# Another order of the last four quarters, Pool scales two of them instead of three, and the row numbers come in two transfers

## The reference

```
x = layer_norm(dense_t @ Wd.T, gd, bd)                         # 2048 x 128
y = layer_norm(einsum('bnd,ed->bne', rows, Ws), gs, bs)        # 26 rows of each sample, 64 -> 128
y = einsum('bne,pn->bep', y, Wsi)                              # 26 features mixed to 32
y = layer_norm(y, gsi, bsi)                                    # over the 32
T = concatenate([x[:, None, :], swapaxes(y, 1, 2)], axis=1)    # 33 vectors of 128
Z = einsum('bnd,bmd->bnm', T, T)                               # all products, lower triangle kept
z = layer_norm(Z[:, tril] @ Wl.T, gl, bl)[:, :384]
h = concatenate([z, dense_t], axis=1)
h = maximum(h @ W_top1 + b_top1, 0)
h = maximum(h @ W_top2 + b_top2, 0)
out = h @ W_top3
```

## Time and profile before

| | us |
|---|---|
| median of 3 runs | 568.91 (567.0 to 570.04) |
| the profiled execution | 569.84 |
| its span, first to last instruction | 568.0 |
| PE busy | 507.3 (89%) |
| DVE busy | 396.6 (70%) |
| Pool busy | 402.7 (71%) |
| ACT busy | 292.3 (51%) |
| mean granted TensorE clock | 0.982 |

### The profile page before, as it was taken

The page is one execution under the profiler, slowest core; times in us unless marked ns, Lnnn a source line. Parts: engine busy times, 40 slices in busy tenths (PEclk is TensorE's granted clock), DMA queues, the critical chain, the costliest instruction groups (busy, mean ns, idle before and its releaser), DMA issues.

```text
span 568.0 us, 20126 instructions
## 1 busy us (share of the span) xinstructions
PE 507.3 (89%) x7271; PEld 380.6 (67%) x7271; DVE 396.6 (70%) x706; ACT 292.3 (51%) x758; POOL 402.7 (71%) x423
## 2 busy tenths in 40 slices
PE   1887869999999999999989899898989899997998
PEld 1854546767677767777676677677667676866576
DVE  4677975877676877768676787767676876675720
ACT  1434565546464655555454545555454654644543
POOL 5777777777777777777777777777777777776310
PEclk9979799999999999999999999999999999998999
DMA  7711221313121221313131221313131221313020
GB/s 250 265 31 28 59 59 30 91 28 93 28 81 39 70 53 28 93 27 92 31 92 28 70 51 35 85 31 91 29 90 32 67 52 29 93 28 90 1 67 2
DMA packets 32138, 36.06 MB, mean 63 GB/s; under 512 B 11789, under 2 KB 20950, under 8 KB 32038
## 3 DMA queue, kind: packets, MB, share of 16 engines
q0 software_dynamic: 13248, 13.65, 12.6%
q1 hardware_dynamic: 18790, 21.11, 11.4%
HBM read 25.54 MB, written 9.18 MB: 61 GB/s over the span
## 4 chain that ended last, share of the span: by engine, by line
POOL 51%; issue 21%; PE 12%; DVE 7%; DMA 4%; ACT 4%; DVEq 0%; ACTq 0%; POOLq 0%
POOL rows L656 51%; DMA rows<-in_table,ids_based 4%; PE bank_z L813 2%; PE bank_b L772 2%; DVE y L432 1%; PE bank_z L745 1%; DVE scaled L394 1%; DVE r_vec L458 1%; DVE y_var L442 1%; PE bank_d L856 1%; PE bank_z L792 1%; PE bank_z L739 1%; PE bank_z L719 1%; DVE scaled L419 1%; PE bank_aw L760 1%
## 5 line engine op out<-in xcount | busy, mean ns | idle before, releaser
L656 POOL DMA_INDIRECT rows<-in_table,ids_based x411 | 394.8, 961 | 128.4 <-issue 122.0
L442 DVE TENSOR_REDUCE y_var<-y_sq 128x32 f32<-128x1024 f32 x63 | 76.9, 1220 | 41.3 <-ACT y_sq L1027 41.2
L1027 ACT ACTIVATE y_sq<-y 128x512 f32<-128x512 f32 x128 | 80.5, 631 | 36.7 <-DVE y L432 36.3
L792 PEld LDWEIGHTS bank_z<-r_vec 128*32 128x32 f32 x4096 | 48.2, 110 | 55.4 <-issue 53.0
L772 PE MATMUL bank_b<-mixed,gs_row 64*128 64x512 f32 x128 | 74.9, 666 | 9.1 <-ACT mixed L1063 7.4
L458 DVE TENSOR_TENSOR r_vec<-y,bank_z 128x512 f32<-128x512 f32 x120 | 77.1, 684 | 2.1
L450 DVE RECIPROCAL bank_z<-y_std 128x32 f32<-128x32 f32 x60 | 21.7, 361 | 77.2 <-ACT y_std L1033 74.0
L813 PE MATMUL bank_z<-wl,zd 128*128 128x512 f32 x160 | 75.2, 615 | 0.0
L745 PE MATMUL bank_z<-gram,rows_t 128*128 128x128 f32 x416 | 65.9, 299 | 10.1 <-ACT rows_t L1048 9.8
L772 PE MATMUL bank_c<-mixed,gs_row 64*128 64x512 f32 x128 | 74.9, 666 | 0.0
L1056 ACT ACTIVATE row_std<-row_var,eps 128x8 f32<-128x8 f32 (+1 forms) x64 | 19.2, 300 | 107.1 <-DVE row_var L403 97.0
(11 more groups left out here) (137 smaller groups left out, 646.3 us busy)
## 6 DMA issues: line engine op xcount, KB each, us to landing
rows<-in_table SPq DMA_DIRECT2D x640, 0.2 KB
zx<-zs SPq DMA_DIRECT2D x15, 560.0 KB
rows<-in_table,ids_based POOLq DMA_INDIRECT x411
dense_t<-in_dense_t SPq DMA_DIRECT2D x1, 2048.0 KB, 8.9
wl<-in_wl SPq DMA_DIRECT2D x1, 1280.0 KB, 12.7
w<-in_w SPq DMA_DIRECT2D x1, 1280.0 KB
zd<-zx SPq DMA_DIRECT2D x15, 80.0 KB
zd<-zx SPq DMA_DIRECT2D x15, 70.0 KB
```

The costliest lines, as they stand in the source:

```text
L442: v.tensor_reduce(y_var[:, k % BANKS, :], y_sq[:, k % 2, :, :].rearrange("e a (s p) -> e (a s) p", p=PROJ), AX_X, ALU.add).then_inc(y_var_ ...
L656: nc.gpsimd.indirect_dma_start(rows[t % ROWS_KEPT][:, c, D * blk:D * (blk + 1)], None, io["table"], bass.IndirectOffsetOnAxis(ap=ids_all[: ...
L792: mm = pe.matmul(bank_i[PROJ * s:PROJ * (s + 1), n * ITEMS:(n + 1) * ITEMS], own[:, Y0:PAD], own, start=True, stop=True)
L1027: nc.scalar.activation(y_sq[:, k % 2, blk, :], y[:, k % 2, blk, :], ACT.Square).then_inc(y_squared, 1)
```

## The change

Four things are changed.

1. The row numbers are two arrays: `ids_first` (the first rows of the tables and the numbers of tile 0, 52 columns) and `ids_rest` (390 columns). SP issues two DMAs, and DVE waits for the second only ahead of the second add.
2. Pool scales y of quarters 61 and 62 only (`POOL_SCALES` is 61); quarter 60 goes through y_reciprocal and y_scale of DVE, as the quarters before it. The mean squares of 61 and 62 are taken in two halves (`y_mean_square_part`).
3. Of the last tile's seven moves Pool does three and SP four (`POOL_MOVES` is 3).
4. The order from turn(62) on is another one on PE, DVE and ACT. The layers of tile 13 stand around the turns of 62 and 63, and the steps of linear(14) later than before.

```diff
+POOL_SCALES = TAIL + 1
+POOL_MOVES = 3
...
             dve.wait_ge(s_ids, 16)
             add_row_base(0, 1)
+            dve.wait_ge(s_ids_rest, 16)
             add_row_base(1, TILES)
...
+            def y_mean_square_part(k, blk):
+                dve.wait_ge(y_squared, 2 * k + blk + 1)
+                dve.wait_ge(y_std_done, k - 3)
+                ins = v.tensor_reduce(y_var[:, k % BANKS, blk * SPB:(blk + 1) * SPB],
+                                      y_sq[:, k % 2, blk, :].rearrange("e (s p) -> e s p", p=PROJ), AX_X, ALU.add)
+                if blk:
+                    ins.then_inc(y_var_done, 1)
...
             y_mean_square(TAIL)
+            y_reciprocal(TAIL)
+            y_scale(TAIL, 0)
+            y_scale(TAIL, 1)
             square_form(TAIL + 2)
             row_mean_square(TAIL + 2)
-            y_reciprocal_kept(TAIL)
             keep_y(TAIL + 1, 0)
...
-            sp.dma_start(ids_based[:], io["ids_based"]).then_inc(s_ids, 16)
+            sp.dma_start(ids_based[:, 0:4 * CHUNKS], io["ids_first"]).then_inc(s_ids, 16)
+            sp.dma_start(ids_based[:, 4 * CHUNKS:], io["ids_rest"]).then_inc(s_ids_rest, 16)
...
-            for k in range(2, BLOCKS):
+            for k in range(POOL_MOVES, BLOCKS):
                 move_in(sp, k, z_moved)
...
-            for k in range(TAIL, QUARTERS - 1):
+            for k in range(POOL_SCALES, QUARTERS - 1):
                 y_scale_pool(k)
...
-            for k in range(2):
+            for k in range(POOL_MOVES):
                 move_in(nc.gpsimd, k, z_moved_last)
...
                 interact(w - 1)
-                first_layer(last - 2, range(0, 2))
+                first_layer(last - 2, range(4))
                 turn(w + 2)
                 mix(w + 1)
                 gram_product(w + 2)
                 project(w + 1)
-                first_layer(last - 2, range(2, 4))
+                second_layer(last - 2, range(0, 2))
+                turn(w + 3)
+                second_layer(last - 2, range(2, 4))
+                gram_product(w + 3)
                 mix(w + 2)
-                turn(w + 3)
-                gram_product(w + 3)
                 interact(w)
                 project(w + 2)
-                linear(last - 1, range(0, 1))
                 mix(w + 3)
+                third_layer(last - 2)
+                project(w + 3)
                 interact(w + 1)
-                project(w + 3)
-                linear(last - 1, range(1, 3))
+                linear(last - 1, range(0, 3))
                 interact(w + 2)
-                linear(last - 1, range(3, STEPS))
+                linear(last - 1, range(3, 4))
                 interact(w + 3)
-                second_layer(last - 2)
+                linear(last - 1, range(4, STEPS))
+                first_dense(last)
                 turn_z(last - 1)
-                first_dense(last)
-                third_layer(last - 2)
                 first_layer(last - 1, range(4))
...
+            relu_1(last - 2)
+            y_root(w)
             keep_turned(w + 2)
+            place_sum_x(last - 1)
             keep_mixed(w + 1)
-            y_root(w)
-            place_sum_x(last - 1)
             row_root(w + 2)
             square(w + 1, 0)
-            relu_1(last - 2)
+            keep_turned(w + 3)
             square(w + 1, 1)
-            keep_turned(w + 3)
+            relu_2(last - 2)
+            row_root(w + 3)
             keep_mixed(w + 2)
```

48 lines of the change are left out of this document (25 added, 23 removed).

## The result

The changed kernel takes **564.94 us** (median of 13 runs, 563.97 to 566.85); the kernel before has a median of 568.91 (13 runs, 567.0 to 571.15). The ratio is 0.9932, with a 95% interval of 0.9917 to 0.9948: faster by 0.5 to 0.8%. The forecast was 565.5.

A forecast was written before the change was run, and what follows sets the result against it. Bound: Pool's unpausing gather queue up to 523.6 us, then the 47.7 us tail from turn(62). Row numbers 0.6, clock and order 3.9, less 0.15 given back, sum to 4.35: 569.84 - 4.35 = 565.5 us; 8-in-10 range 564.6 to 568.4.

The forecast's parts named there:

- forecast case: The whole kernel as predicted, with the clock staying at 1.00 in the tail: 564.7 to 566.4 us, chance 60%.
- Row numbers: At the kernel's start, a smaller first transfer lets Pool's gathers begin sooner: 0.6 us gained, range 0 to 0.8.
- The holes: PE's waits in the tail: 1.1 or 1.2 us left ahead of turn(62), 0.5 us ahead of turn(63).
- The clock: Behind turn(62), the granted clock stays at 1.00 instead of 0.50 for 6.8 us: up to 3.4 us gained.
- rival 1: Behind the tail's holes the clock falls once, for a shorter 3.4 us: 566.9 us, chance 18%.
- The order itself: PE's new sequence up to interact(63), apart from the clock: 0.5 us of the 3.9 us gained there.
- From interact(63) to the last linear: Late tail, round trip through memory: 9.2 us against 9.04 before, giving back 0.15 us.
- the landing of Pool's third move: Last step of the round trip ahead of the last linear: 2.6 us from the move to landing.
- PE's own path: PE's work from interact(63) through first_layer(14): ends about 8.4 us after interact(63) starts, covered by the round trip.
- the 0 of the prediction: Final chain, linear 15 to the stored rows: same instructions, so 0 us change.
- DVE and Pool: Tail: y_scale(60) moved to DVE is free if y_root(60) comes in time, 1.5 us cost otherwise; adds nothing to the sum.
- Rival 3: Clock falls at PE's new holes late in the tail: alone 568.9 us, 5%; with an earlier long fall 571.9, 4%.

The follow-up runs named there:

- after_again: The changed kernel as it is, timed again on another chip as reference: median 565.20 us, ratio 0.9917.
- before_idle_fill: The kernel before with six unused identity matmuls added behind the first half of first_layer(13), ahead of turn(62): 568.08 us, ratio 0.9979.
- before_first13: The kernel before with only first_layer(13) moved whole ahead of turn(62): 570.23 us, ratio 1.0012.
- before_full_fill: The kernel before with ten unused identity matmuls added in the hole ahead of turn(62): 566.98 us, ratio 0.9956.
- before_ids: The kernel before with the row numbers in two transfers and nothing else: 568.88 us, ratio 0.9993.
- after_two_moves: The changed kernel with two of the seven last moves on Pool instead of three: 565.24 us, ratio 0.9936.
- after_hole: The changed kernel with five of the twelve matmuls of first_layer(13) left out, widening the hole ahead of turn(62): 566.97 us, ratio 0.9966.
- after_root_early: The changed kernel with the root of y's last half put ahead of keep_z(62) on ACT: 565.05 us, ratio 0.993.
- after_fill: The changed kernel with five unused identity matmuls added behind first_layer(13), ahead of turn(62): 564.75 us, ratio 0.9911.
- after_pool60: The changed kernel with y of quarter 60 scaled by Pool again instead of DVE: 565.29 us, ratio 0.9934.
- after_no_ids: The changed kernel with the row numbers in one transfer again: 566.12 us, ratio 0.9944.
- after_root_fill: The changed kernel with the root of y's last half ahead of keep_z(62) and five unused matmuls ahead of turn(62): 565.78 us, ratio 0.9939.

## Why the prediction was right, step by step

The time came out 0.6 us under the forecast and within the forecast case (564.7 to 566.4); no rival took over. The parts were right too, but for the last stretch before the final linear step, and the reason given for the clock was weaker than the outcome makes it look.

**Row numbers, 0.6.** The two profiled executions show 0.57 us, the means over all of them 0.75, and the medians can't tell better than 0.3 to 0.9. The Trainium skill, DMA: Bandwidth & Descriptors, section "Anatomy of one DMA — SWDGE (gpsimd) path", gave an estimate of 0.45. That fit is for transfers of the GpSimd path, and this one is issued by SP; the measured starts lie above it. The DMAs behind the second transfer are issued 0.47 us later (bs_row at 4.81 instead of 4.34), and no gather waits for them.

**The holes, 1.2 and 0.5.** Measured 1.41 and 0.48 (after_again 0.96 and 0.66). turn(63) starts 2.46 us behind the start of the last gather, where 2.5 was forecast (522.69 to 525.2). The first depends on Pool's queue: the gathers of one execution aren't those of the next.

**The clock, 3.4.** To see its size apart from how early quarter 62 comes, take each profiled execution's time less the start of turn(62):

| execution | order | time less turn(62) | low clock behind it |
|---|---|---|---|
| before | old | 569.84 - 520.26 = 49.58 | 6.8 us |
| before_idle_fill | old | 567.14 - 519.16 = 47.98 | 3.4 us |
| before_first13 | old but for first_layer(13) | 566.81 - 519.82 = 46.99 | 3.4 us, behind the hole ahead of mix(62) |
| before_full_fill | old | 565.80 - 519.38 = 46.42 | none |
| before_ids | old | 565.74 - 519.36 = 46.38 | none |
| after_two_moves | new | 566.08 - 519.74 = 46.34 | 3.4 us |
| after_hole | new | 566.90 - 520.71 = 46.19 | 3.4 us |
| after | new | 564.77 - 518.92 = 45.85 | none |
| after_root_early | new, one swap on ACT | 565.39 - 519.59 = 45.80 | none |
| after_again | new | 565.26 - 519.74 = 45.52 | none |
| after_fill | new | 565.44 - 519.93 = 45.51 | none |
| after_pool60 | new | 564.46 - 518.97 = 45.49 | none |
| after_no_ids | new | 565.13 - 519.73 = 45.40 | none |
| after_root_fill | new, one swap on ACT | 566.13 - 521.02 = 45.11 | none |

In the old order the long fall costs 49.58 - 46.40 = 3.2 us and the short one 1.6: the 3.4 and 1.7 of the prediction within 0.2. In the new order, without the two swapped kernels, the short one costs only 0.3 to 0.9 us (46.19 and 46.34 against 45.40 to 45.85), since the wait ahead of turn(63) takes up part of it; rival 1 had allowed 0.3 us for that and put the cost at 1.4. What the prediction left out of its sum is that 3.2 us is the price of one execution. In the medians the filled kernel gains 2.5 us. That the fall doesn't come in every execution, nor always at its full length, would explain it, and the profiles of before_ids (no fall) and before_idle_fill (the short one) are examples; how often it comes isn't counted. The prediction said that some runs may have a shorter slow stretch, and put the gain against the median at 3.4 us; the measured 3.97 lies between that and the 4.35 of the sum.

The reason for a clock of 1.00 was that both new holes are shorter than the hole of 1.67 us that had left it there. As a rule this doesn't hold: holes of 1.46 us (before_idle_fill) and 1.41 us (after_two_moves) were followed by a fall. That none follows the same 1.41 us in the changed kernel's profile is in part luck. Of the eight profiled executions with the new order and nothing left out, one had a fall, the short one; the 18% of rival 1 were a fair chance.

**The order itself, 0.5.** 46.40 less the new order's 45.40 to 45.85 is 0.55 to 1.0 us. The medians of the two filled kernels, timed on one chip, give more: 566.98 less 564.75 is 2.2 us, 0.75 of them the row numbers, so 1.5 us for the order, with an interval of about 1.2 us to either side of each. interact(63) starts 5.0 us sooner: 0.57 is the start, 0.58 Pool's chance, and 3.85 are left for clock and order together, against 3.9 predicted.

**From interact(63) to the last linear, 9.2 against 9.04: the term that was mis-sized.** Both numbers were. Before, the row of the last linear starts at 552.28, and the prediction took 552.44, the modelled end of first_layer(14): the stretch was 8.88 us long (552.28 - 543.40). After the change it is 8.88 as well (547.28 - 538.40). It gives nothing back, where 0.15 was forecast. In the sum of the round trip the step that failed is the landing of Pool's third move, put at 2.6 us. It took 2.3:

```profile
DMA to landing us min/median/max: 2.3/2.3/2.3
```

With that the prediction's own steps give 8.9. The trip was the bound in this execution, as forecast, but only just: it held the last linear for 0.2 us (3.01 us from start to start, against 2.79 before). In after_again and after_pool60 it didn't, and PE's own path took 8.42 and 8.43 us, as reckoned (8.4):

```profile
545.07 2.94 PE L872 MATMUL bank_b<-z_t,w 128*128 128x128 f32 x24 [1.25 <-ACT z_t L1125]
547.85 4.56 PE L829 MATMUL bank_z<-wl,zd 128*128 128x512 f32 x10
```

The swap in after_root_early was enough to make the trip the bound again. From the last linear to the end of the span both kernels take 15.72 us, the 0 of the prediction. Sized right, this term moves the sum from 4.35 to 4.5, and Pool's 0.58 makes it 5.1 where the profiled executions differ by 5.07.

**DVE and Pool.** y_scale(60) was free, as reckoned, and after_pool60 shows that it needn't have been moved: scale_rows(62) is slow there, 1.73 us, and the tail isn't longer for it.

**The sum against the medians.** Row numbers 0.3 to 0.9, order 0.55 to 1.0, clock 2.5: 3.4 to 4.4 us, and 3.97 were measured. The clock's 2.5 has an interval of 1.1 to 3.9, so this sum agrees with the result but doesn't fix the shares.

**The rivals.** Rival 1, the short fall, didn't show in the changed kernel's own profile nor in after_again, but it did in after_two_moves, which differs in one constant. It comes with some executions, and no difference of PE's instructions there decides it. Rival 3, a fall late in the tail, showed nowhere in the changed kernels. The rule of the Trainium skill, TensorE: Matmul & The Clock Gate, section "What's actually happening", that activity lifts the clock, speaks for the fills, which are work without use. Ten matmuls did what it says, in their profile no fall is left; six did so by half, a fall of 3.4 us remained in theirs. By that rule the prediction had rival 1, whose fall came in one of eight executions.

**What stays open.** What decides between a fall and none. Holes of 0.66 to 1.19 us ahead of turn(62) were followed by none (six executions: after_root_fill, after_again, after_pool60, after_no_ids, before_full_fill, before_ids), those of 2.45 and 2.54, and the 1.99 ahead of mix(62) in before_first13, by one; a hole of 1.41 us was followed by either, one of 1.46 by a fall. How often the clock falls in the runs that were only timed isn't shown directly. Their mean clock is 0.978 before (first two batches) and 0.984 after; 0.006 of 565 us is 3.4 us of full clock, the size of one long fall, but it says nothing of where in the program. after_root_fill has the low mean of 0.976 and no fall between 519 and 533 in its profile, and over the 63 runs of the kernel before the correlation of time with lost clock is only 0.36. A fall earlier in the program has Pool's queue as cover, and may cost nothing: the profiled execution of after_pool60 has 20.5 us of low clock, all of it before 430 us, and at 564.46 us it is the shortest of all. That wasn't tested by itself. And two profiled executions of one kernel, the changed one, are few: the differences between the others are those of one execution each.

## What to carry to other kernels

A short idle of TensorE ahead of late data can cost more than itself: read the granted clock behind each hole in the part that sets the end, and try to fill the hole with real work from elsewhere, or, if there is none, with matmuls that nobody reads. Moving one block forward only moves the hole, unless what it leaves behind is filled too, so follow the wait that comes next before counting the gain. And where a gain rests on something that comes and goes between executions, one profiled execution can show its full price (3.2 us here) while the median shows less (2.5), so time many runs before giving the gain a size.
